# Router logits with the gate weights on the fixed side, and VectorE's layer-norm work moved ahead of the router

## The reference, cut to what matters

```python
x = layernorm(x + attn(x))                       # attn: tok[n] * value_row[c] for each sequence
scores = softmax(xf @ gate_w.T)                  # 4096 x 8
top_vals, top_idx = top_k(scores, 2)             # two experts per token, weights = top_vals
eo = (y * silu(g)) @ W2[e].T                     # y, g = split(xf @ W1[e].T); H = 192
z = sum over the two experts + gated_mlp(xf, Ws1, Ws2)   # the shared expert, hidden width 384
return layernorm(x + z)
```

## Time and profile before

| what | us |
|---|---|
| median of 3 runs | 352.89 |
| lowest and highest run | 350.03, 357.9 |
| profiled execution, first to last instruction | 354.0 |
| busy: PE, DVE, ACT, POOL | 315.3, 265.5, 192.7, 197.5 |
| group stage, groups 2 to 7 on TensorE | from 82.94 to 180.45 |

### The profile page before, as it was taken

One profiled execution on the slowest core, in us unless ns is written; L12 is line 12 of the kernel. 1 busy time (PEld: TensorE's weight loads), 2 busy tenths in 40 slices (PEclk: granted clock), 3 DMA queues, 4 the chain that ended last, 5 costly groups with the idle time before them and its releaser, 6 DMA issues.

```text
span 354.0 us, 7780 instructions
## 1 busy us (share of the span) xinstructions
PE 315.3 (89%) x2225; PEld 282.8 (80%) x2225; DVE 265.5 (75%) x1037; ACT 192.7 (54%) x425; POOL 197.5 (56%) x223
## 2 busy tenths in 40 slices
PE   2879899999999989999989979999999999999700
PEld 1446788789888878888889979999999999999600
DVE  0886679866989897966686765676678886988785
ACT  1043686646657362733335644555655566868862
POOL 4048750746778858667271542444757675686620
PEclk9969999999999999999999998999999999999955
DMA  7967420212371202442124643444899797789758
GB/s 221 378 220 262 126 62 0 95 47 75 101 216 58 92 33 93 114 136 101 35 98 140 191 144 100 129 131 131 178 247 204 202 243 190 177 236 252 204 189 324
DMA packets 31383, 54.63 MB, mean 154 GB/s; under 512 B 4880, under 2 KB 22544, under 8 KB 31344
## 3 DMA queue, kind: packets, MB, share of 16 engines
q1 hardware_dynamic: 23136, 29.82, 28.1%
q0 software_dynamic: 8208, 24.32, 23.9%
HBM read 29.73 MB, written 24.40 MB: 153 GB/s over the span
## 4 chain that ended last, share of the span: by engine, by line
PE 48%; DVE 16%; DMA 12%; SPq 8%; POOL 6%; issue 4%; ACT 4%; POOLq 0%; DVEq 0%; ACTq 0%
PE bank L1062 15%; PE bank L946 10%; PE bank L1088 8%; PE bank L968 4%; DMA stage<-ws_t 4%; PE bank L931 3%; PE bank L1071 3%; DMA stage<-rows_in 3%; PE bank L1031 3%; DVE xs L1174 3%; DVE htlo L1379 2%; SPq L415 2%; DVE mix L1374 2%; POOL rows_in L560 2%; POOL w1lo L516 2%
## 5 line engine op out<-in xcount | busy, mean ns | idle before, releaser
L600 POOL DMA_INDIRECT rows_out<-stage,place x71 | 69.4, 977 | 67.2 <-ACT stage L769 51.8
L560 POOL DMA_INDIRECT rows_in<-x,slot x64 | 65.3, 1020 | 47.1 <-DVE slot L1289 30.6
L749 ACT ACTIVATE stage<-bank 128x384 f32<-128x384 f32 (+1 forms) x36 | 17.5, 486 | 43.7 <-PE bank L1062 43.7
L1062 PE MATMUL bank<-w1hi,xthi 128*128 x142 | 39.8, 362 | 1.3 <-DVE xs L1385 1.1
L769 ACT ACTIVATE stage<-bank,weight 128x256 f32<-128x256 f32 x71 | 30.0, 471 | 15.8 <-PE bank L1088 15.7
L1062 PE MATMUL bank<-w1hi,xtlo 128*128 x142 | 36.9, 341 | 0.0
L1062 PE MATMUL bank<-w1lo,xthi 128*128 x142 | 36.8, 340 | 0.0
L1391 DVE TENSOR_TENSOR xtlo<-bank,xthi 128x512 fp32r<-128x512 f32 (+1 forms) x36 | 24.3, 676 | 13.7 <-ACT xthi L695 13.4
L1519 DVE TENSOR_TENSOR stage<-bank,stage 128x384 f32<-128x384 f32 (+1 forms) x36 | 19.8, 551 | 18.6 <-ACT stage L749 18.5
L687 ACT ACTIVATE mix<-bank 128x512 f32<-128x512 f32 x24 | 14.2, 591 | 34.1 <-PE bank L946 34.1
L946 PE MATMUL bank<-xthi,ws1hi 128*128 128x512 f32 x96 | 31.3, 407 | 0.0
(11 more groups left out here) (242 smaller groups left out, 893.4 us busy)
## 6 DMA issues: line engine op xcount, KB each, us to landing
stage<-rows_in SPq DMA_DIRECT2D x71, 133.0 KB, 2.6
xs<-rows_out POOLq DMA_DIRECT2D x12, 512.0 KB, 6.5
xs<-x SPq DMA_DIRECT2D x8, 512.0 KB, 9.2
out<-xs SPq DMA_DIRECT2D x7, 512.0 KB, 5.4
stage<-w_t SPq DMA_DIRECT2D x8, 384.0 KB, 4.4
rows_in<-clear SPq DMA_DIRECT2D x16, 133.0 KB
rows_out<-stage,place POOLq DMA_INDIRECT x71, 3.3
stage<-w_t SPq DMA_DIRECT2D x2, 512.0 KB, 3.9
```

Of the source, the lines that this page charges most:

```text
L560: pool.indirect_dma_start(rows_in[0:E * CAP, :], bass.IndirectOffsetOnAxis(slot[:, q * G + t, k:k + 1], 0), x2[q % 2][:, t, :], None).then ...
L600: pool.indirect_dma_start(rows_out[:, :], bass.IndirectOffsetOnAxis(place[:, 2 * j + b:2 * j + b + 1], 0), by[j % 4][:, b * C:(b + 1) * C] ...
L749: act.activation(bsg[j % 2][:, 0:width(j)], bank_h[j % 2][:, 0:width(j), H:F], ACT.Silu).then_inc(s_bsg, 1)
L1062: mm = pe.matmul(bank_h[j % 2][:, b, 0:F], bx[j % 2][:, (2 * b + k) * P:(2 * b + k + 1) * P], w[:, bass.ds(e, 1), k, :], start=(a == 0), s ...
```

## The change

In groups 2 to 7 the logits are made the other way round. `logits_of_rows` (TensorE) has the 16 gate columns on the fixed side and streams all 512 tokens past them: four products instead of sixteen, with the result turned (16 rows of 512). `logits_copy` (ScalarE, first in its group, ahead of `high`) copies it from PSUM to a free piece of `stage`. `logits_back` (TensorE) turns it back with four transposes, and stands behind `first_layer(g, 0)`. The layout that VectorE reads is the same as before, so `route` is unchanged.

On VectorE, in the same groups, all four attention additions of group g + 2 and `inverse_std(g + 1)` come before `route(g)` instead of between the later steps.

```diff
+        logits_t = work[:, 3 * RING:3 * RING + GT]
+        def turned(g):
+            return 2 <= g < NG
...
+            def logits_copy(g):
+                act.wait_ge(s_ltp, g - 1)
+                act.activation(logits_t[0:2 * E], banks[2][0:2 * E], ACT.Copy).then_inc(s_lt, 1)
...
             for g in range(NG):
+                if turned(g):
+                    logits_copy(g)
                 if 2 <= g <= 3:
                     high(6 + g)
                 silu(g, 0)
...
+            def logits_of_rows(g):
+                pe.wait_ge(s_slot, g)
+                pe.wait_ge(s_xt, g + 1)
+                steps = [(xt, k) for xt in (xthi, xtlo) for k in range(KC)]
+                for a, (xt, k) in enumerate(steps):
+                    mm = pe.matmul(banks[2][0:2 * E, :], gate[:, k].rearrange("p h e -> p (h e)"), xt[:, k, :],
+                                   start=(a == 0), stop=(a == len(steps) - 1))
+                mm.then_inc(s_ltp, 1)
+
+            def logits_back(g):
+                pe.wait_ge(s_lt, g - 1)
+                for t in range(G):
+                    mm = pe.transpose(banks[2][:, t * 2 * E:(t + 1) * 2 * E], logits_t[0:2 * E, t * P:(t + 1) * P],
+                                      ident[0:2 * E, 0:2 * E])
+                mm.then_inc(s_lg, 1)
...
             def group(g):                       # TensorE
-                logits_of(g)
+                if turned(g):
+                    logits_of_rows(g)
+                else:
+                    logits_of(g)
                 first_layer(g, 0)
+                if turned(g):
+                    logits_back(g)
...
             def group(g):                       # VectorE
                 after = g + LN_AHEAD
+                if turned(g):
+                    if after < NG:
+                        layer_norm(after, range(G))
+                    if g + 1 < NG:
+                        inverse_std(g + 1)
                 route(g)
                 tables(g)
...
                 product(g, 0)
-                if g != 1 and g + 1 < NG:
+                if g != 1 and g + 1 < NG and not turned(g):
                     inverse_std(g + 1)
...
-                elif g > 1 and after < NG:
-                    layer_norm(after, range(0, 2))
                 slots(g)
...
-                if g > 1 and after < NG:
-                    layer_norm(after, range(2, G))
                 if g:
                     hidden_lo(g, 2)
```

More of the change, by code:

```diff
@@ L254, in post_norm_layer @@
         s_lg, s_m = sem("logits"), sem("chosen")
+        s_ltp, s_lt = sem("logits_t_psum"), sem("logits_t")
         s_pos, s_slot, s_sc = sem("positions"), sem("slots"), pair("scattered")
```

## The result

| | before | after |
|---|---|---|
| median of four runs each, taken together, us | 352.78 | 363.95 |
| lowest and highest run | 350.03, 357.9 | 360.97, 366.92 |
| ratio, 95% interval | | 1.0227 [1.0134, 1.032] |
| profiled execution, first to last instruction | 354.0 | 359.2 |
| group stage, groups 2 to 7 on TensorE | 97.5 | 106.9 |

The kernel became slower: 2.3% by the ratio, with an interval of 1.3 to 3.2%, so that it is slower is clear of the noise, and that it is so by more than 2% is not. The forecast was 362 us. The medians lie 11 us apart and the ratio says some 8 us, because two of the four runs after are slow ones (a state that some executions fall into) and the ratio takes the fast runs alone.

What follows compares the result with a forecast made beforehand. TensorE was taken to bound the group stage. Late router less vanished gaps +1.6, GpSimd hold-ups +4.4 and clock falls +3.1 us summed to +9.1, giving 362 us on the median, range 354 to 367.

Steps and rivals of the forecast that it cites:

- A: Late router, GpSimd hold-up and clock falls all together: 362 us, own range 359 to 367; chance 0.50.
- steps 1 to 4: Group stage: later starts of the first layer's third piece cost 4.5 us, vanished gaps save 2.9; together +1.6 us.
- step 5: GpSimd's weight work holds up VectorE's table steps: 2.0 us in group 3, 1.2 in groups 4 and 5; +4.4 us.
- Step 1: Logits on TensorE: four products 0.94 us, four transposes 0.45; TensorE's own work falls by 0.3 us a group.
- Step 2: ScalarE's copy, about half a us, lies under the first piece and costs nothing; uncovered 0.6 us a group.
- Step 3: VectorE's router starts later, so the first layer's third piece waits for product(g, 0); sum 4.5 us later.
- 7.1 + X: Start of the first layer's third piece, in us into the group; X is the time of VectorE's table steps.
- Step 4: VectorE's additions and root steps ahead of the router are hidden; TensorE's 2.9 us of second-layer gaps go.
- Step 6: TensorE's idle time in groups 3 to 5 drops its clock; two falls taken, +3.1 us.
- B: VectorE's small table steps are not held up, no clock fall, gaps of 1.0 to 1.6 us: 354.5 us; chance 0.25.
- C: VectorE's table steps are held up but TensorE's clock stays: about 359.5 us; chance 0.15.
- D: VectorE's product(g, 0) comes in time, TensorE never waits behind places: -4.8 us, 348 us; chance 0.07.

Runs made afterwards that it cites:

- the kernel without reads: Changed kernel with GpSimd's subtractions for weight pieces 6 to 9 replaced by clears: 358.82 us, ratio 1.0115 to the kernel before.
- the run with the clock held up: Changed kernel with unused constant products on TensorE in the idle time of groups 3 to 5: 359.78 us, ratio 1.0167 to the kernel before.

## Why the prediction was right

Its likeliest case, A, came about: +9.4 us of stage against a sum of +9.1. The mechanism is the forecast one, but that the sums agree so closely is partly luck: steps 1 to 4 came out 1.8 us lower than forecast and step 5 2.5 us higher.

**The base.** The device time of the profiled execution is 1.8 us over its span of 359.2, so the one before, 354.0 by its span, was some 1.8 us more. The prediction took 354.0 for its time. This did no harm: it is added and taken off again, and 352.9 + 9.1 is 362 either way.

**Step 1, right.** Logits rows 0.92 us for the four (0.94 forecast); the transposes 0.36 in the chain (0.45 forecast, below the low end of 0.42).

**Step 2, right.** No wait of PE for the copy stands in the waits after.

**Step 3, right in kind.** Router 4.22 us into group 3 (4.37 forecast), tables at 6.22 (6.38). Without hold-up the third piece starts about where 7.1 + X puts it: in group 6 7.61 (7.85), and in group 3 of the kernel without reads 8.62 (8.75).

**Step 4, right, and worth more than said.** In group 3 additions and root steps were done at 102.22, 0.63 us before the router. The waits in front of the second layer are gone. The stretch behind the third piece came to 8.0 us, not 8.3: in the earlier trace rows the gap at 147.39 is the one seen, but another was hidden. From the start of the eight transposes to that of the next piece it is 1.10 us in group 5 before (144.28 to 145.38) and 0.79 in the rows at 113.52 above. The piece waits for VectorE's `htlo`, which ended at 145.32; the kernel before has, on VectorE and on TensorE:

```profile
144.63 0.69 DVE L1379 TENSOR_TENSOR htlo<-mix,hthi 128x512 fp32r<-128x512 f32 x1
...
145.38 0.39 PE L968 MATMUL bank<-ws2hi,hthi 128*128 128x256 f32 x1
```

So the 0.3 us were a wait that overlapping matmuls cover up, and no idle time is shown for it. The gaps were about 0.8 us a group instead of 0.49, and steps 1 to 4 came to -0.2 us (what is left of +9.4 without steps 5 and 6) instead of +1.6.

**Step 5, right in kind, too small.** The hold-ups came to about 0.95, 1.9, 2.1 and 2.0 us in groups 2 to 5, the start of the third piece into the group (8.45, 10.61, 11.69, 10.50) less the one forecast without a hold-up (7.5, 8.75, 9.6, 8.5): 6.9 us against 4.4. The term that failed in size is the one for group 2, put at nothing without a reason, though the weight work comes there too (6.8 us into the group): its two table steps took 0.75 and 0.65 us instead of 0.17 under the weight work, which the trace has from 89.13.

```profile
88.53 0.75 DVE L1340 SCALAR_TENSOR_TENSOR tc<-begin,above 128x8 f32<-128x8 f32 x1
89.31 0.65 DVE L1341 TENSOR_SCALAR ends<-tc 128x8 f32<-128x8 f32 x1
```

And in groups 4 and 5 it was 2.1 and 2.0, not 1.2 each: in group 4 five steps of 0.58 to 0.74. The rule that both operands must be in SBUF was too narrow as well, and the trace before could tell: among the four root steps beside the weight work is one with a single input, held like the others.

```profile
123.06 0.66 DVE L1185 TENSOR_SCALAR rn<-rn 128x4 f32<-128x4 f32 x1
```

The Trainium skill, SBUF — State Buffer, section "Who interferes with whom", holds a step with two SBUF inputs against a GpSimd instruction that reads SBUF and not against one that only writes. The run with clears agrees for `entry`, 0.22 us beside the clear and 0.62 beside the subtraction. Its exemption for a single input outside the two-port modes did not help here: a `tensor_scalar` took 0.65 us beside a subtraction and 0.86 and 1.50 beside clears, while one at 126.95 in group 4 passed in 0.16 during the subtractions. The page counts `tensor_scalar` among those that can enter such modes, which would explain it, but no run here showed the mode.

**Step 6, right in kind, one fall, not two.** In this trace only group 4's clock fell: pairs of products at 1.06 us instead of 0.62, the window 131 to 132 at 0.50 of 2.4 GHz, that is 1.2 GHz. Behind the third piece's start the group took 10.7 us instead of 8.0: 2.7 us for one fall, against 1.6 put on it. The granted clock stood at 0.50 from 128.2 to 134.6 there, twice as long as behind the gap in the trace before (210.9 to 214.2). Run again, groups 3 and 4 fell, and group 3's fall cost 1.6 us (9.54 behind the third piece's start against 7.98). So 2.7 against 3.1 agrees, but not by the two falls that were forecast.

**The sum.** -0.2 + 6.9 + 2.7 = +9.4 us, against +1.6 + 4.4 + 3.1 = +9.1.

**The stage behind.** It was taken to move as a whole and came out 3.6 us shorter in this trace (173.55, then 169.99), which is why the two profiled spans lie only 5.2 us apart while the medians lie 11.2 and 9.9 apart. It is no gain of the change, as far as the runs tell: the kernel before ran again had 170.5, and among the other runs' profiles on the chips where the kernel before takes about 354 us it lay between 168.1 and 172.1 us. The before trace had the 2.06 us gap with its half clock, the after trace a 1.6 us gap and no fall behind it.

**The rivals.** B is excluded by the 0.63 to 0.76 us steps. C is what the run with the clock held up is: 359.78 us where the kernel before took 354.13, and 359.5 forecast on 352.9. D, product in time, needed the table steps elsewhere: with them ahead of the router it comes in time, and the kernel took 349 us, where D had 348.

## What to carry to other kernels

When work is moved to later on one engine, write down who waits for what stands behind it in line, not only for it: here the logits were in time for `places`, and the short steps behind the router held up the piece after it. Short VectorE steps that read SBUF belong where no GpSimd element work can lie on them, and GpSimd's work moves when what releases it moves. A wait shown as none can still lie inside overlapping matmuls, so compare the distances of starts between a stretch that waits and one that doesn't.

## What the runs showed of the hardware

- A `tensor_scalar` on 8 or 16 numbers a partition (0.17 us alone) took 0.86 and 1.50 us beside a GpSimd clear, to the end of all four clears, and a cast of four numbers 1.61 us, while two-input steps took 0.22 and 0.18 us beside such clears when no single-input step stood before them.
- The same wait does not always drop TensorE's clock: 3.34 us left it at 1.00 in one execution and 3.31 us dropped it in the next; 0.75 and 1.49 us, with four short products between, dropped it in a third. A fall cost 1.6 us where the clock stood at 0.50 for some 3.3 us (and group 3 of the change run again), and 2.7 where it did for 6.4.
- The kernel before took 361 us on one chip and about 354 on three others, and its relation to a variant moved from 0.989 to 1.004 with it.
